# Bias rows in the keys of the first attention, and one root for a norm of a norm

## The reference, cut to what matters

```python
def _L0_xattn_ref(memory, query, b, seq_len):            # 16 heads of 8
    k_mem, v_mem = jnp.split(memory, 2, axis=2)
    Q = _split_heads(query, 16) * 8 ** (-0.5)
    Kh, Vh = _split_heads(k_mem, 16), _split_heads(v_mem, 16)
    logits = jnp.einsum('bhqd,bhkd->bhqk', Q, Kh) + b    # b: one number for each key
    valid = (jnp.arange(S)[None, :] < seq_len[:, 0:1]).astype(jnp.float32)
    logits = logits + MASK_VALUE * (1.0 - valid)[:, None, None, :]      # -1e12
    weights = jax.nn.softmax(logits, axis=-1)
    return jnp.einsum('bhqk,bhkd->bhqd', weights, Vh)
...
x = x + jnp.tanh(g_xattn[0]) * _L0_xattn_ref(ctx_2048, _layernorm(x), L0_xattn_b, seq_len)
x = x + jnp.tanh(g_ffn[0]) * _L0_ffn_ref(_layernorm(x), ...)
x = x + jnp.tanh(g_xattn[1]) * _L1_xattn_ref(_layernorm(x), ctx_2048, ...)   # keys of the context and its own
...
# layer 3: the norm of a norm, both over the 128 features, eps 1e-5
h = rmsnorm(_layernorm(x), g_res)
```

## Time and profile before

| | |
|---|---|
| runs | 2059.64, 2062.75, 2069.62 us; median 2062.75 |
| profiled execution | 2063.91 us; its span 2062.1 us |
| busy | TensorE 1650.3 us (80%), VectorE 1209.1 (59%), ScalarE 1042.4 (51%), POOL 686.4 (33%) |
| mean granted TensorE clock | 0.841 |
| HBM | 119.67 MB read, 80.74 MB written |
| chain that ended last | TensorE 19%, POOL 7%, VectorE 6%, DMA 5%, issue 4% |

### The profile page before, as it was taken

The page is one execution under the profiler, slowest core; times in us unless marked ns, Lnnn a source line. Parts: engine busy times, 40 slices in busy tenths (PEclk is TensorE's granted clock), DMA queues, the critical chain, the costliest instruction groups (busy, mean ns, idle before and its releaser), DMA issues. The chain is left out here.

```text
span 2062.1 us, 42577 instructions
## 1 busy us (share of the span) xinstructions
PE 1650.3 (80%) x14902; PEld 1071.9 (52%) x14902; DVE 1209.1 (59%) x3694; ACT 1042.4 (51%) x2171; POOL 686.4 (33%) x1196
## 2 busy tenths in 40 slices
PE   1788997999998999868998996667577688788544
PEld 0333444677665666544444665555344477676332
DVE  3454555544436889845887655454665542366666
ACT  1344443433325777644554563534344565486556
POOL 4343310120003333212555312731667430541460
PEclk9995558999997999978999998888755698898756
DMA  7544426630005555331222211353745122321100
GB/s 198 127 92 110 120 58 184 205 82 1 0 1 125 127 133 142 73 111 44 68 64 62 75 49 63 91 143 96 191 100 129 57 67 71 107 87 39 45 26 21
DMA packets 191504, 184.65 MB, mean 90 GB/s; under 512 B 26528, under 2 KB 174944, under 8 KB 189984
## 3 DMA queue, kind: packets, MB, share of 16 engines
q1 hardware_dynamic: 182288, 145.22, 27.1%
q10 hardware_dynamic: 816, 19.92, 3.2%
q0 software_dynamic: 8192, 16.79, 2.9%
HBM read 119.67 MB, written 80.74 MB: 97 GB/s over the span
## 5 line engine op out<-in xcount | busy, mean ns | idle before, releaser
L2209 DVE TENSOR_REDUCE mneg<-psb 128x4 f32<-128x512 f32 (+1 forms) x576 | 383.3, 684 | 206.2 <-PE psb L1803 198.7
L2583 ACT ACTIVATE HB<-psb 128x512 f32<-128x512 f32 x384 | 218.7, 596 | 147.5 <-PE psb L1803 143.5
L1803 PE MATMUL psb<-K,Q 48*128 48x128 bf16 (+1 forms) x1280 | 192.5, 265 | 114.0 <-DMA Q<-sc_q 44.5
L1803 PE MATMUL psb<-Q,K 51*128 51x128 bf16 (+2 forms) x1664 | 267.2, 301 | 5.5 <-ACT HB L2583 2.3
L2802 POOL TENSOR_SCALAR rs<-mv 128x2 f32<-128x2 f32 (+1 forms) x96 | 21.9, 229 | 654.7 <-DVE mv L2169 652.4
L1803 PEld LDWEIGHTS psb<-K,Q 48*128 48x128 bf16 (+1 forms) x1280 | 111.8, 113 | 204.7 <-issue 134.6
L2583 ACT ACTIVATE HB<-psb,bias 128x512 f32<-128x512 f32 x192 | 131.2, 685 | 169.5 <-PE psb L1803 168.6
L1803 PEld LDWEIGHTS psb<-Q,K 51*128 51x128 bf16 (+2 forms) x1664 | 177.1, 138 | 29.7 <-issue 11.6
L1803 PE MATMUL psb<-HB,VA 128*9 128x128 f32 (+1 forms) x2560 | 164.0, 340 | 5.2 <-ACT OE L2588 4.7
L1803 PE MATMUL psb<-KS,Q 48*128 48x128 bf16 x1024 | 140.0, 228 | 25.6 <-DMA Q<-mT 11.3
L1803 PE MATMUL psb<-biasT,selbb 96*128 96x512 bf16 x192 | 109.9, 572 | 0.0
(11 more groups left out here) (480 smaller groups left out, 3816.6 us busy)
## 6 DMA issues: line engine op xcount, KB each, us to landing
K<-sc_k SPq DMA_DIRECT2D x96, 192.0 KB, 3.7
Q<-sc_q SPq DMA_DIRECT2D x96, 192.0 KB
tok_rows<-in_zero ACTq DMA_DIRECT2D x16, 1152.0 KB, 32.8
sc_q<-comp SPq DMA_DIRECT2D x48, 192.0 KB, 2.2
K<-tok_rows SPq DMA_DIRECT2D x72, 128.0 KB, 2.1
sc_q<-comp SPq DMA_DIRECT2D x48, 128.0 KB, 2.1
vraw<-in_ctx SPq DMA_DIRECT2D x48, 128.0 KB, 4.7
KS<-sc_s SPq DMA_DIRECT2D x32, 192.0 KB
```

The costliest lines, as they stand in the source:

```text
L1803: return pe.e.matmul(out, w, x, start=start, stop=stop, skip_group_check=True)
L2209: t = e.tensor_reduce(m.mneg[:, s.b % 4, s.i * A.per:(s.i + 1) * A.per], PSB[s.use.bank].rearrange("p (h k) -> p h k", h=A.per), AX.X, ALU ...
L2583: a.done(act(m.HB[:, s.slot, :], PSB[s.use.bank], ACT.Exp, bias=bz), s.use.drained)
```

## The change

The bias of the first attention gets three rows of its own in the keys: rows 48 to 50 of K hold the three bf16 parts of the bias of each key, and Q has ones there; the maxima and their ones move to rows 51 to 53. The scratch arrays `sc_k` and `sc_q1` get 51 rows of 16 heads (`longer`). Once at the start SP stores the bias parts into `sc_k` (six DMAs, after the turned bias is there) and zeros into `sc_q1` (three DMAs), so that in the second attention rows 48 to 50 of K's tile, whatever they hold, are multiplied by zero. `rows_load` reads 51 partitions a half where the source is `sc_k` in the first attention, or `sc_q1`, the Q of the second; the second attention's loads of K and KS, and the first one's of Q, keep 48. The product with `biasT` and the bias operand of the exponential are gone from the first attention; the third keeps both. Q8's places are set to one at the start like K8's: two more memsets on VectorE, two more on POOL.

The norm of a norm takes one inverse root, of var x (1 + eps) + eps x eps. Two guesses of the planner change with this.

```diff
-        "norm_in": lambda: (("dve", 450 * s.n), ("pool", {None: 2000 if s.rms else 1600, "second": 3200, "both": 4100}[s.twice])),
+        "norm_in": lambda: (("dve", 450 * s.n), ("pool", {None: 2000 if s.rms else 1600, "second": 3200, "both": 1900}[s.twice])),
-        "scores": lambda: (("pe", (230 if not s.beside else 130) + (220 if A.bias_i is not None or A.causal else 0)), ("dve", 720)),
+        "scores": lambda: (("pe", (230 if not s.beside else 130) + (220 if A.bias_i is not None and not A.bias_rows or A.causal else 0)), ("dve", 720)),
...
-        self.scratch = {n: scratch(n) for n in ("sc_k", "sc_q0", "sc_q1", "sc_q3", "sc_s")}
+        self.scratch = {n: scratch(n) for n in ("sc_q0", "sc_q3", "sc_s")}
+
+        self.longer = {n: nc.dram_tensor(n, [NP, 51 * 16, 256], BF16, kind="Internal").ap() for n in ("sc_k", "sc_q1")}
+        self.scratch |= {n: a[:, 0:768, :].rearrange("p (c q) t -> p c q t", c=6) for n, a in self.longer.items()}
...
-        self.n_rows, self.halves = (96, 1) if dh == 16 else (48, 2)
+        self.n_rows, self.halves = (96, 1) if dh == 16 else (51, 2)
+
+        self.bias_rows = bias_i is not None and dh != 16
...
-    k8_free[0], k8_free[1] = inc("dve", "clear_dve"), inc("dve", "clear_dve")
+    q8_free[0], k8_free[0], q8_free[1], k8_free[1] = (inc("dve", "clear_dve") for _ in range(4))
     t_const = inc("dve", "consts")
-    k8_free[2], k8_free[3] = inc("pool", "clear_pool"), inc("pool", "clear_pool")
+    q8_free[2], k8_free[2], q8_free[3], k8_free[3] = (inc("pool", "clear_pool") for _ in range(4))
...
     do("setup", cst=t_cst, ints=t_i, g=t_g, cols=t_cols, uses=biasu)
+    do("bias_store", need=t_biasT)
+    t_bias_rows = dma("dma_bias", 6)
+    t_zero_rows = dma("dma_zeros", 3)
...
-                tk = load_rows(A, "K8", "k8", "sc_k", p, (k_in[p], k8_free[A.at(p)]))
+                tk = load_rows(A, "K8", "k8", "sc_k", p, (k_in[p], k8_free[A.at(p)], t_bias_rows if A.bias_rows else None))
...
-            tq = load_rows(A1, "Q8", "q8", "sc_q1", p, (got["q"], q8_free[A1.at(p)]))
+            tq = load_rows(A1, "Q8", "q8", "sc_q1", p, (got["q"], q8_free[A1.at(p)], t_zero_rows))
...
-        if A.bias_i is not None:
+        if A.bias_i is not None and not A.bias_rows:
             t = matmul(o4, m.selbb[:, s.b:s.b + 1].broadcast_to([96, 128]), m.biasT[:, A.bias_i, :].unsqueeze(1).broadcast_to([96, 4, 128]),
                        False, True, False)
...
-        s["last"] = s.A.bias_i is None and not s.A.causal
+        s["last"] = (s.A.bias_i is None or s.A.bias_rows) and not s.A.causal
...
-            v.done(e.memset(m.place(m.K8, i), 1.0), ("clear_dve", i + 1))
+            v.done(e.memset(m.place(m.Q8, i), 1.0), ("clear_dve", 2 * i + 1))
+            v.done(e.memset(m.place(m.K8, i), 1.0), ("clear_dve", 2 * i + 2))
...
-        if A.bias_i is not None:
+        if A.bias_i is not None and not A.bias_rows:
             a.wait_ge(s.bias)
             bz = m.bias[:, A.bias_i, s.b:s.b + 1]
         a.done(act(m.HB[:, s.slot, :], PSB[s.use.bank], ACT.Exp, bias=bz), s.use.drained)
...
-        ones(m.K8, 2, count())
-        ones(m.K8, 3, count())
+        for at in (2, 3):
+            ones(m.Q8, at, count())
+            ones(m.K8, at, count())
...
-        else:
+        elif s.twice != "both":
             then(e.tensor_scalar(r0, var, EPS, None, ALU.add))
-        if not s.twice:
+        if s.twice == "both":
+
+            then(e.tensor_scalar(r0, var, 1.0 + EPS, EPS * EPS, ALU.mult, ALU.add))
+        if s.twice != "second":
             if s.by == "act" and not s.rms:
                 then(e.tensor_tensor(r1, r0, power, ALU.pow))
                 shift()
...
+            rows = sc[p].rearrange("c (d h) t -> (c d) h t", d=A.dh)
+            if s.sc == "sc_q1" or s.sc == "sc_k" and A.bias_rows:
+                rows = m.longer[s.sc][p].rearrange("(r h) t -> r h t", h=16)
+            n = rows.shape[0]
             for half in range(2):
-                src = sc[p].rearrange("c (d h) t -> (c d) h t", d=A.dh)[:, 8 * half:8 * half + 8, :]
-                load(name, dst[64 * half:64 * half + 6 * A.dh, :].rearrange("r (h t) -> r h t", h=8), src)
+                load(name, dst[64 * half:64 * half + n, :].rearrange("r (h t) -> r h t", h=8), rows[:, 8 * half:8 * half + 8, :])
...
+    def bias_store(s):
+
+        sp.wait_ge(s.need)
+        rows = m.longer["sc_k"][:, 768:816, :].rearrange("p (c h) t -> p c h t", c=3)
+        zero = m.longer["sc_q1"][:, 768:816, :].rearrange("p (c h) t -> p c (h t)", c=3)
+        for c in range(3):
+            for b in range(2):
+                src = m.biasT[32 * c + b:32 * c + 32:2, 0, :].unsqueeze(1).broadcast_to([16, 16, 128])
+                load("bias", rows[:, c, :, 128 * b:128 * b + 128], src)
+        for c in range(3):
+            load("zeros", zero[:, c].bitcast(F32), io["zero"][0:16, :])
```

## The result

The changed kernel took 2147.43 us (median of 4 runs, 2140.45 to 2157.64), the kernel before 2061.19 (4 runs, 2047.69 to 2069.62) beside it: ratio 1.0429, 95% interval 1.0354 to 1.0503. It is slower by 86 us, where 2049 us were forecast. The profiled execution took 2142.78 us, its span 2140.9.

What follows compares the result with a forecast made beforehand. TensorE's columns were taken to bound the first attention, with the loop of row maxima close behind. The sum was 2063.9 - 33 + 8.5 + 13 + 2 - 4.5 = 2049.9, against the median 2049 us; range 2006 to 2085.

Steps and rivals of the forecast that it cites:

- three engines: Loads of 51 rows in both attentions: carried by three of 16 engines, with Q<-mT queued behind on the same ones; chance 0.52.
- the upper bound: Longer loads of K and Q: at three engines of 22 GB/s each, a half takes 3.1 us.
- the step without the bias product: First attention: a step of score and weight products and sums takes 1.09 us at a clock of 0.50.
- the double norm of 2.0 us: Tail: POOL's norm of a norm takes 2.0 us, not 4.3.
- the store's own time: Storing maxima behind slow loads: nothing added in the first attention after the engines come free, 0.2 us in the second.
- the -33 for the steady pairs: First attention: 15 pairs take 14.0 us each against 16.2, with odd maxima 1.3 us late.
- four forced pauses of +2.1 each: First attention, up to 193 us: maxima directly behind K's load on SP's queue wait 2.1 us more, four times: +8.5.
- The second attention: Maxima behind Q's slow loads are late by 1.0 us in the mean over 13 pairs: +13 us.
- the rival in which the clock falls: Second attention: each late maximum also lowers TensorE's clock, costing 13 x (1 + 3) = +52 us; total 2088, chance 0.20.
- the first attention's -24.5: First attention as a whole: forecast 24.5 us shorter, steady pairs -33 and pauses +8.5.
- The rival with the full clock: First attention: with loads harmless, TensorE rises to 2.4 GHz, a pair takes some 11.8 us, -66; total 1994, chance 0.03.
- Start and tail: Start: new stores delay the first store of parts, +2 us (0 to +8); tail: one root per double norm, -4.5 us.

Runs made afterwards that it cites:

- e1: The changed kernel with each load of 51 rows split into two, of 48 and 3 rows; ratio to the kernel before 0.9979.
- e3: The changed kernel with scratch and loads of 52 rows in place of 51, still one DMA a half; ratio to the kernel before 1.0006.
- e2: The changed kernel with the planner's two guesses, for scores and double norm, put back; ratio to the kernel before 1.0357.
- e11: e7 with the planner's old guess for the scores; ratio to the kernel before 0.9885, first attention 243.3 us.
- e12: e7 with ScalarE issuing the first attention's maxima for the first 18 batches only; ratio to the kernel before 0.9871, first attention 235.4 us.
- e7: The changed kernel with 48-row loads, K's bias rows in small DMAs, Q's zeros loaded once a place, bias stores behind weights; ratio to the kernel before 0.9938.
- e5: The changed kernel with the second attention's Q loads back at 48 rows a half, zeros left out; ratio to the kernel before 1.0186.
- e4_norm: The kernel before with only the norm's edit, one root for a norm of a norm, and its planner cost; ratio to the kernel before 1.0008.

## Why the prediction was wrong

Of the 93 us between the sum (2049.9) and the profile (2142.8) 55 lie in the first attention, 39 in the second, 6 in the start and 2 in the feed-forward part; the tail takes 9 back.

**Right: three engines.** The choice of the upper bound, 3.1 us a half, was right (share 0.19; 74 GB/s make it 2.8), as was the queue behind it; so were the step without the bias product (1.08 us, 254.20 to 255.28, where 1.09 was drawn) and the double norm of 2.0 us.

**Wrong: the store's own time.** The sum let the odd maxima be there when the three engines come free, 8.7 us after K's issue, or 0.2 later. The engines were free nearly as drawn: the last packet of K's and Q's loads starts 9.0 us after K's issue (260.17), and the packets of the maxima follow, from 260.49 to 260.93. But they are used only at 261.72, 10.6 us after K's issue (251.15). So 1.5 us lie between the free engines and the use, where the sum had 0.2. An unhindered store has some time behind its data too: the even batch's, issued at 249.57, has its packets from 250.93 to 251.82 and is used at 252.25. In the second attention the use came 11.4 us after Q's issue, where 8.9 was taken:

```profile
769.25 0.90 SPq L2857 DMA_DIRECT2D Q<-sc_q  x2
...
780.67 0.26 PE L1812 MATMUL psb<-K,Q 51*128 51x128 bf16 x1 [2.84 <-issue]
```

So the odd batch of a steady pair was 2.9 us late, not 1.3, and the pair took 16.4 us, not 14.0; the rest of these 2.4 us are short waits for ScalarE (0.4) and steps that don't lie as drawn. Of the -33 for the steady pairs 9 us are left over the whole stage, pauses aside.

**Wrong: four forced pauses of +2.1 each.** There were six of 8.5 to 13.8 us, 40 us more than before in place of 8.5. Most of that needs no slow load: with fast ones the pauses of over 4.5 us still make 53 us (e1) and 50 (e3), so of the 40 some 25 remain. The planner's lower guess for the scores explains only 3 to 5 of them (e2, e11). That the others come from the faster steps, which reach the same preparation sooner while the maxima stand behind its stores and loads on SP's queue, is argued; e12, in which they don't stand there for the first 18 batches, is 20 us shorter than e7.

**The second attention** was a term of the sum mis-sized: +13 forecast, +52 measured, +47 by e1 and +51 by e5. It is the rival in which the clock falls, with its price, 13 x (1 + 3); the split between pause and clock was off (34 us of waits, not 13). The rival's total, 2088, fell short because it took the first attention's -24.5 over, which was +30.6.

**The first attention's gain** failed at a row used for more than it shows. A clock of 0.50 over 124 us was one execution; in four of six the clock rises and the bias product lies beside little. Against those, a change with fast loads gains nothing there (248.3 and 247.0 against 245 to 250), and the change itself costs 50 us there, not 31. The rival with the full clock looked at the kernel after only. The Trainium skill ("TensorE: Matmul & The Clock Gate", Part 1), by which activity releases the throttle, was set aside on that one stretch. Four other profiles bear it out in part: the throttle is released there, but only behind stretches of 8 to 65 us in which TensorE was wholly busy.

**Start and tail**: +7.8 for +2 (inside the bound of 8, by slow first loads and late stores together). The new stores took SP 0.66 and 0.62 us each (18.76 and 22.76 above), not 0.45 to 0.55. The tail's norm is -2 to -11 for -4.5. Of the bias products eight, not nine, run before 64.3 us, which moves nothing.

## What to carry to other kernels

Before adding rows to a DMA, look at what the new count divides by: 51 rows ran on 3 engines, 52 on enough that nothing was lost, and the price fell on small transfers issued at about the same time or later, by whatever engine. A store has time of its own ahead of its data and behind it, and the part behind doesn't vanish under a wait for the DMA engines. And where a stage runs at the lower clock in one profile, take a second one before pricing TensorE's columns there.

## What the runs showed of the hardware

A load of 51 x 8 x 256 bf16 moved at 74 GB/s with a share of 0.19; one of 52 rows cost nothing to be seen. Maxima of 12 KB that ScalarE issued 0.4 us ahead of such loads by SP had their packets among those of the loads and were used 9.4 us after their issue; with nothing in the way it was 2.7. The kernel of before ran its first attention at 0.50 from 142 us to the end (e4_norm) or nearly so (before), and in four other profiles had 41 to 58 us at the full clock from 198 to 255 us on, which made it 20 us shorter. And the same program took some 115 us more on some chips than on others, nearly all of it behind 900 us.
